# Scatters of edge codes that wait, two at a time, for the blocks of a projection on a one-core graph network kernel

## What is computed

```python
x = _layernorm(x + _L0_gnn_ref(...))          # attention, 4 heads
# L1: top-32 sparsified neighbours, mean over incoming edges
h_sparse = _maxk(feat @ W_neigh, 32)
neigh = segment_sum(h_sparse[src], dst) / maximum(deg, 1)
x = _layernorm(x + feat @ W_self + neigh)
# L2: 16 relations, forward (to dst) and backward (to src)
proj = einsum('ni,rio->rno', x, Wf)           # 3125 x 256 -> 16 tables
m_forward = segment_sum((proj[etypes, src] + bias) * norm_f, dst)
m_backward = the same with Wb, src and dst exchanged
x = _layernorm(x + 2 * x @ loop + bias + m_forward + m_backward)
x = _layernorm(x + _L3_gnn_ref(...))          # two attention layers over src
```

## Time and profile before

| | |
|---|---|
| median of the runs | 7348.49 us |
| span of the profiled execution | 8945.4 us |
| busy: PE, DVE, POOL | 57%, 51%, 58% of the span |
| last gather of e1 issued | 2831.7 us |
| scatters issued | 2833.0 to 3246.5 us |
| `project_out` blocks | 2881.4 to 3567.2 us |
| first gather of e2f | 3574.0 us |

### The profile page before, as it was taken

The page is one execution under the profiler, slowest core; times in us unless marked ns, Lnnn a source line. Parts: engine busy times, 40 slices in busy tenths (PEclk is TensorE's granted clock), DMA queues, the critical chain, the costliest instruction groups (busy, mean ns, idle before and its releaser), DMA issues.

```text
span 8945.4 us, 80437 instructions
## 1 busy us (share of the span) xinstructions
PE 5070.2 (57%) x17709; PEld 3398.4 (38%) x17709; DVE 4560.5 (51%) x11322; ACT 1221.8 (14%) x4092; POOL 5223.0 (58%) x5325
## 2 busy tenths in 40 slices
PE   4444444455554159677776655556555556555555
PEld 2333332222232024344444433325555545554554
DVE  5665567666663014444444333335555555555555
ACT  3555552000000000000000000002111112111112
POOL 4666661566666730666666666664666654666664
PEclk7776777677766579788888766667777777677777
DMA  3222221333322025444444333332222223222222
GB/s 83 47 48 47 46 47 30 87 91 90 89 80 62 19 70 166 136 133 134 132 133 112 90 90 90 91 90 75 81 83 83 83 80 76 81 81 82 81 81 68
DMA packets 499429, 753.18 MB, mean 84 GB/s; under 512 B 217891, under 2 KB 351257, under 8 KB 498713
## 3 DMA queue, kind: packets, MB, share of 16 engines
q0 software_dynamic: 236352, 604.00, 24.3%
q1 hardware_dynamic: 262616, 144.15, 5.6%
HBM read 622.95 MB, written 124.79 MB: 84 GB/s over the span
## 4 chain that ended last, share of the span: by engine, by line
PE 30%; another core or an unknown queue 23%; issue 20%; DVE 12%; SPq 8%; POOL 3%; DMA 2%; DVEq 2%; ACT 1%; POOLq 0%; ACTq 0%
PE ps L301 17%; SPq L1429 7%; DVE acc L289 5%; PE ps L2019 4%; PE ps L926 3%; POOL rows L249 3%; PE ps L1319 2%; PE ps L1310 2%; DVE onehot L270 1%; DMA rows<-table2b,slots_s 1%; DVEq L275 1%; DVEq L289 1%; DVE top L519 1%; SPq L1425 1%
## 5 line engine op out<-in xcount | busy, mean ns | idle before, releaser
L289 DVE TENSOR_TENSOR acc<-acc,ps 128x257 f32 (+3 forms) x4992 | 1880.3, 377 | 2656.2 <-remote 1460.7
L301 PE MATMUL ps<-rows,onehot 128*128 128x257 f32 (+1 forms) x4992 | 1845.6, 504 | 1435.6 <-issue 714.6
L249 POOL DMA_INDIRECT rows<-table,slots_d x1664 | 1631.7, 981 | 1050.6 <-issue 485.2
L301 PEld LDWEIGHTS ps<-rows,onehot 128*128 128x128 f32 x4992 | 1069.0, 239 | 2272.3 <-issue 1312.9
L301 PE MATMUL ps<-msg,onehot 128*128 128x136 f32 (+1 forms) x4992 | 1258.1, 414 | 740.1 <-remote 374.1
L301 PEld LDWEIGHTS ps<-msg,onehot 128*128 128x128 f32 x4992 | 1003.8, 259 | 973.5 <-issue 816.1
L249 POOL DMA_INDIRECT rows<-table2f,slots_d x832 | 804.0, 966 | 764.7 <-DMA table2f<-big 326.5
L249 POOL DMA_INDIRECT rows<-table3b,slots_s x832 | 828.0, 995 | 538.6 <-DVE msg L1372 283.2
L249 POOL DMA_INDIRECT rows<-table3a,slots_s x832 | 828.5, 996 | 526.3 <-DVE msg L1372 274.3
L249 POOL DMA_INDIRECT rows<-table2b,slots_s x832 | 798.2, 959 | 437.6 <-issue 225.0
L1319 PE MATMUL ps<-big,msg 128*128 x3328 | 635.4, 351 | 631.3 <-issue 433.6
(11 more groups left out here) (310 smaller groups left out, 4185.7 us busy)
## 6 DMA issues: line engine op xcount, KB each, us to landing
table2f<-big SPq DMA_DIRECT2D x80, 640.0 KB
table2b<-msg SPq DMA_DIRECT2D x200, 256.0 KB
rows<-table,slots_d POOLq DMA_INDIRECT x1664
slots_d<-recs_d SPq DMA_DIRECT2D x832, 2.5 KB
rows<-table2f,slots_d POOLq DMA_INDIRECT x832
rows<-table2b,slots_s POOLq DMA_INDIRECT x832
rows<-table3a,slots_s POOLq DMA_INDIRECT x832
rows<-table3b,slots_s POOLq DMA_INDIRECT x832
```

Of the source, the lines that this page charges most:

```text
L249: nc.gpsimd.indirect_dma_start(out=rows[:, j, 0:width], out_offset=None, in_=table[:, :], in_offset=bass.IndirectOffsetOnAxis(ap=slots[:, ...
L289: nc.vector.tensor_tensor(acc[:, bass.ds(b * width, width)], acc[:, bass.ds(b * width, width)], ps[:, bank + k, 0:width], ALU.add).then_in ...
L301: nc.tensor.matmul(ps[:, bank + k, 0:width], onehot[:, h, k, :], rhs, start=True, stop=True).then_inc(sem(of(s, "tile_sum")), 1)
```

## The change

Every second scatter gets one more wait: scatter `i` (even) may only be issued when `pf_ev` has reached `i * 175 // 314`, rounded down. So scatters 0 and 1 are free, scatter 2 waits for the first finished projection block, scatter 4 for the second, 10 for the fifth, and the last two, 312 and 313, for block 173 of 200.

```diff
         BATCH = 16
         NBATCH = -(-(NCH + NSG) // BATCH)
+        PLACED_TO = NB * PAIRS - NB
 
         def place_codes(pool):
...
                 if i % BATCH == 0:
                     after(pool, f"gs_placed{n % 2}", 16 * BATCH * (n // 2))
+                if i % 2 == 0:
+                    after(pool, "pf_ev", i * PLACED_TO // (NCH + NSG))
                 if i < NCH:
                     rows_out, at, what = codes, to_c[:, i:i + 1], kept[:, i * CHUNK:(i + 1) * CHUNK]
```

## The result

| | median | runs |
|---|---|---|
| before | 7348.05 us | 6, from 7345.13 to 7369.44 |
| after | 7370.99 us | 6, from 7363.03 to 7386.82 |

The ratio is 1.003, 95% interval 1.0019 to 1.004: the changed kernel is slower by 22.9 us, where +20 was forecast.

A forecast was written before the change was run, and what follows sets the result against it. The prediction took POOL's scatters (415 us) to bound the stage, ending 30 us after the projection. First gate +20, waits 0, later gates 0 and less crowding 0 gave 7348.5 + 20 = 7368 us; range 7285 to 7450.

The forecast's parts named there:

- The stretch is not in the runs: Projection beside the scatters: its slowing in the 8945.4 us profile was taken as mostly absent from the timed runs.
- The argument from room: Whole kernel: of 1597 us profile surplus, gather stages can give 1183, so 414 must come from elsewhere.
- Waits cost 0: POOL's scatters: the added wait instructions themselves cost 0, at most 47 us if each cost an issue gap.
- First gate 20 us: Scatter 2 on POOL now waits for the first projection block: 20 us taken, 46.5 by the profile.
- Later gates 0, at most 2 us: Scatters after the first gated pair: POOL is as slow as its gates, then slower; 0, at most 2 us.
- The scatters last by 30 us: End of the stage: scatters end at 3248, the projection at 3218, so scatters set the next stage's start.
- The sum: Whole kernel: +20 us on the scatter chain that ends the stage, moving all behind it; 7368 us.
- Hidden: Rival, chance 0.25: projection ends after the scatters even when they start 20 us late; 7348 us, give or take 10.
- Freed: Rival, chance 0.20: the scatter flood really stretches the projection and pacing removes that; -212 us, 7136, or 7295 at a quarter.
- The prediction's sign that the first 25 blocks come at 2 to 3 us: Projection in the changed profile: that pace would mean the earlier profile's stretch came from the scatter backlog.
- Taking turns: Rival, chance 0.15: scatter pairs and projection blocks run in sequence; +324 us, 7672, or +108, 7456, with a third so.
- a packet's turn: DMA queues: engines alternate by packet, so a scatter backlog costs another queue only its turn; no gain for projection stores.

The follow-up runs named there:

- met waits: The kernel before, with every second scatter waiting on `e0_done`, reached long before: 157 waits, no gate; 7350.17 us, ratio 1.0002.
- e1: Not a run: a gather stage of the kernel; the lengths read from each profile start at its last gather. No time of its own is given.
- late gates: The kernel before plus the change's pacing set 40 blocks behind, so 74 scatters are free; 7347.18 us, ratio 1.0001.
- first gate at block 12: The kernel before plus one wait only: scatter 2 waits for the twelfth projection block; 7403.17 us against 7364.15, ratio 1.0056.
- gates 10 behind: The changed kernel with each wait's block count lowered by 10, so scatters 0 to 19 are free; 7360.84 us against 7356.62, ratio 1.0.

## Why the prediction was right

The forecast was +20 us, 7368 us, with 7285 to 7450 as the range; 7370.99 was measured. The first gate was the predicted cost and had the right size. Two other terms were off in opposite directions and nearly cancel, and the kernel before has another wait last than the prediction said. That the sum is within 3 us is in part luck.

- *The stretch is not in the runs.* Right. The argument from room (1597 us had to come from somewhere, and the gather stages could give only 1183) is borne out: no later profile has it. The bound of 647 us for the stage held, measured 422; and so did the conclusion that it is near what its scatters need (415).
- *Waits cost 0.* Right, shown by 157 met waits. (The change adds 156, not 157: a count of 0 makes no wait.)
- *First gate 20 us.* 21.2 above the gap in the changed kernel, 23.0 where it stood alone. The time from the last gather to the first `pf_ev`, estimated from the earlier trace rows as 2855.6 - 2831.7 = 23.9, measured 2504.3 - 2479.5 = 24.8.
- *Later gates 0, at most 2 us.* This term was mis-sized: it measured 10.9 us in the changed kernel and 6.9 in the one with the single codes first. The step took 2.3 us for each of the first 25 blocks, from the shortest transpose of the earlier trace rows (0.27 us; the median is 0.418) and matmuls at full clock. They took 2.65 us each, and the first 17, which is as far as the gates were closed, 3.05. What is lost is read at the last closed gate: scatter 32 waits for block 17, which starts 48.9 us after block 1, while the 30 scatters from the first gate on need only 30 x 1.28 = 38.4 us. At 2.3 us a block the gate would have been open. The clumps split the loss over seven gates, and the faster blocks behind the 17th don't give it back.
- *The scatters last by 30 us.* Mis-sized, and the path was wrong by the prediction's own sign: it called its sum wrong if e2f's first gather follows a store. In the kernel before it does, at a wait of 8.3 us. The projection's end was forecast 386 us after the last gather of e1 (3218 - 2831.7), and the stage without single codes took 392.3, so the undisturbed chain was estimated to within 6 us. What was missing is that the single codes lengthen it by 30 us: 11.7 in the blocks, 17.7 in the last store's landing (23.7 - 6.0; 13 to 14 in the profiles of the late gates and the met waits).
- *The sum.* In the profiles: the scatter chain, from its first start to its last end, grows from 412.7 to 447.9 us, 35.2. Of that 32.2 are the closed gates, and 3 are a little more of the waits for a batch. At e2f's first gather the 8.0 us that POOL waited for the store beyond an ordinary gap are absorbed, and the stage grows by 27.2. At the 17th, 13.2 are: the read-back starts 18.3 us after the last scatter's end before and 9.1 in the changed kernel, and takes 10.2 and 6.3. So G grows by 35.2 - 13.2 = 22.0, E by 25.4, the timed runs by 22.9. (The two spans differ by 37.5 us; 13.7 of them lie ahead of the last gather of e1, where nothing was changed.) Twenty from one term was really 35 less 13.

Differences to the kernel before, us:

| kernel | stage | G | timed median |
|---|---|---|---|
| the change | +27.2 | +22.0 | +22.9 |
| first gate alone | +17.0 | +11.6 | +8.4 |
| first gate at block 12 | +44.8 | +39.0 | +39.0 |
| late gates, 40 behind | -1.9 | -0.6 | -1.1 |
| met waits | -5.8 | 0.0 | +1.9 |
| gates 10 behind | -5.3 | +0.8 | +4.2 |
| without the single codes | -30.0 | -31.8 | -22.5 |
| single codes first | -0.6 | -13.4 | -18.5 |
| the change, single codes first | +25.8 | +12.5 | +10.1 |
| single codes in the middle | -13.1 | -25.8 | -19.4 |

G follows the timed runs within 4 us where the scatters keep their order and within 10 elsewhere; the stage can be 18 us off.

The rivals. *Hidden* is true for 9 of the 35 us, by a delay of the last store, as that rival had it; 4 more are the shorter read-back, which nobody had foreseen. *Freed* is rejected: with the change the blocks take 371.9 us from first to last (2503.6 to 2875.5), the same as before (2491.8 to 2863.7), and the 40-blocks-behind gates gain nothing. The prediction's sign that the first 25 blocks come at 2 to 3 us proves nothing for it: they do so without the change too (59.6 us for the 24 behind the first). *Taking turns* is rejected as well: in the 374 us from 2554 us to the last scatter no gate was closed.

That a packet's turn is all that a backlog of scatters costs another queue, which the prediction took from the Trainium skill (DMA: Bandwidth & Descriptors, Queues, rings and completion order), agrees with the chunks (360.8 us of blocks with 32 of them, 360.2 with 202) and not with the single codes (371.9). The same page, under Specifications, says that pieces under 512 B make the DMA engine read, modify and write. Chunks of 16 bytes and codes of 4 are both under it, and only the latter cost the stores anything here, so the rule alone doesn't account for it. Why the single codes do was not found.

## What to carry to other kernels

Pacing one queue by another's progress costs as much as the pacer is ever behind: compare, gate by gate, when the release comes with when the queue would have got there by itself, and take the largest difference. A mean over the whole stage, or a block's time taken from its shortest parts, hides it. A gate set some steps behind avoids most of it (ten blocks here left 6.7 us, which didn't show in the time). What a delay is then worth is read where the next engine runs out of work, here at the 17th gather of e2f and not at the first. Before pacing at all, look at which transfers disturb the neighbour, and when: here moving a third of the scatters away from the last store and the read-back won 0.25 to 0.3% without a wait, where pacing all of them lost 0.3%. And when a profile's span is far over the median, take a second profile before trusting any idle time in it; if there is none, place the surplus by what the other stages can give.

## What the runs showed of the hardware

- One execution of 8945.4 us had waits for "remote" on DVE, ACT, PE and POOL, of which 1460.7 us at a single line. None of the twelve later profiles of this kernel and its variants has any among its 200 costliest groups of waits, and eleven of the twelve spans lie between 7329 and 7401 us. What made it is open.
- Where single codes go out beside stores, the DMA engines are busy and move little. Ten-us windows of the kernel before, profiled again (columns as in the earlier trace rows; the single codes begin at about 2726, and their last 30 are under way from about 2837):

```profile
2735.00:2745.00 10.00, 10.00 (x25) 4.40 (x24) 2.76 (x4) 0.00 (x0) 7.56 (x9) 1.00 1.16 116
...
2795.00:2805.00 10.00, 10.00 (x25) 4.40 (x24) 4.15 (x6) 0.00 (x0) 7.56 (x9) 1.00 0.57 179
...
2827.00:2837.00 10.00, 10.00 (x25) 4.47 (x24) 3.85 (x7) 0.00 (x0) 7.56 (x9) 1.00 0.49 145
2837.00:2847.00 10.00, 10.00 (x25) 4.46 (x24) 3.13 (x5) 0.00 (x0) 7.58 (x8) 1.00 0.89 151
2847.00:2857.00 10.00, 9.70 (x23) 4.10 (x22) 3.08 (x5) 0.00 (x0) 7.75 (x8) 1.00 0.91 115
2857.00:2867.00 10.00, 4.24 (x10) 1.52 (x8) 3.08 (x5) 0.00 (x0) 7.66 (x8) 0.88 1.22 120
2867.00:2877.00 10.00, 0.00 (x0) 0.00 (x0) 0.00 (x0) 0.00 (x0) 7.56 (x9) 0.50 0.94 116
```

The share comes out above 1 in two of these short windows. It doubles, from 0.49 or 0.57 to 0.89 and more, while the rate falls to between 151 and 115 GB/s; DVE's blocks stop with the store that they wait for. With the single codes in the middle, the end of the projection has chunks beside it:

```profile
2866.00:2876.00 10.00, 10.00 (x24) 4.40 (x24) 4.14 (x6) 0.00 (x0) 7.56 (x9) 1.00 0.44 133
```

Only two parts of the single codes raise the share, roughly the first 30 and the last 30 to 40 of the 112, and not the stretch between. With the single codes first, the first part goes out before any store exists and is free; the second is over 260 us before the end of the stage. That matches the times, but no run varied the parts by themselves.
- POOL's brake, that a batch of 16 waits until the batch two before it has landed, costs 12 us in the kernel before, 11.1 of it ahead of one scatter, 40 us behind the first single code. Without the single codes one wait of 1.7 us is left. No run removed the brake.
- Gathers through codes that mostly weren't written took 1.60 us each (1330 us for 832) instead of 1.26, with DVE and PE named as their releasers. The cause wasn't looked for.
